# Window attention kernel: first scores in one burst of 32-row matmuls per half image, and a new order of work on all engines

## What is computed

```python
win = x.reshape(B, C, nH, w, nW, w).transpose(0, 2, 4, 3, 5, 1).reshape(B * nH * nW, S, C)
q, k, v = jnp.split(_layernorm(win, ln1_g, ln1_b) @ in_w.T + in_b, 3, axis=-1)   # then split into 8 heads
scores = jnp.einsum('bhsd,bhtd->bhst', q, k) / jnp.sqrt(jnp.float32(dh))
attn = jax.nn.softmax(scores, axis=-1)
o = jnp.einsum('bhst,bhtd->bhsd', attn, v)
win = win + o @ out_w.T + out_b                                                  # y1
h = _layernorm(y, ln2_g, ln2_b)
y = y + jax.nn.silu(h @ fc1_w.T + fc1_b) @ fc2_w.T + fc2_b                       # y2
# second layer, per image: (wo (q k / N) v) is folded into one 128x128 matrix M
out = M @ y2 + d
```

## Time and profile before

| | |
|---|---|
| median of 3 runs | 365.84 us (365.79 to 366.97) |
| profiled execution | 366.59 us, of which the span of the trace is 364.8 us |
| TensorE busy, weight loads busy | 348.3 us (95%), 299.3 us (82%) |
| VectorE busy | 285.1 us (78%) |
| ScalarE busy | 245.6 us (67%) |
| GpSimd busy | 166.9 us (46%) |
| mean granted clock of TensorE | 0.988 |

### The profile page before, as it was taken

The page is one execution under the profiler, slowest core; times in us unless marked ns, Lnnn a source line. Parts: engine busy times, 40 slices in busy tenths (PEclk is TensorE's granted clock), DMA queues, the critical chain, the costliest instruction groups (busy, mean ns, idle before and its releaser), DMA issues. The chain is left out here.

```text
span 364.8 us, 9920 instructions
## 1 busy us (share of the span) xinstructions
PE 348.3 (95%) x3424; PEld 299.3 (82%) x3424; DVE 285.1 (78%) x850; ACT 245.6 (67%) x449; POOL 166.9 (46%) x177
## 2 busy tenths in 40 slices
PE   7899899999999999999999999999999999999875
PEld 6788788888888888888888888878888888878563
DVE  5676888888788878798788888888788878867652
ACT  5557776775959477674968658684877659684360
POOL 6513575444455434635445433646444443622430
PEclk9999999999999999999999999999999999999995
DMA  4242130303222131302123031212123031210011
GB/s 133 67 100 63 33 97 4 91 29 82 76 60 72 29 86 58 86 29 72 63 67 86 14 101 58 70 45 58 58 72 101 0 86 58 60 31 2 0 60 58
DMA packets 31859, 21.99 MB, mean 60 GB/s; under 512 B 22432, under 2 KB 23776, under 8 KB 31840
## 3 DMA queue, kind: packets, MB, share of 16 engines
q1 hardware_dynamic: 31744, 21.62, 21.7%
q10 hardware_dynamic: 96, 0.13, 0.1%
HBM read 4.95 MB, written 4.19 MB: 25 GB/s over the span
## 5 line engine op out<-in xcount | busy, mean ns | idle before, releaser
L526 POOL TENSOR_TENSOR hid_l<-hid,hid_h 128x512 fp32r<-128x512 f32 x30 | 40.4, 1369 | 37.1 <-ACT hid_h L1136 35.3
L706 PE MATMUL p_score<-kd_h,qd_h 128*128 128x128 f32 (+1 forms) x512 | 55.8, 252 | 1.6 <-DMA qd_h<-q_h 1.5
L706 PEld LDWEIGHTS p_score<-kd_h,qd_h 128*128 128x128 f32 (+1 forms) x512 | 49.9, 163 | 6.9 <-DVE row_max L1344 1.7
L1102 ACT ACTIVATE probs<-p_scoreT 128x512 f32<-128x512 f32 x64 | 38.6, 603 | 24.5 <-PE p_scoreT L729 24.4
L1344 DVE TENSOR_REDUCE row_max<-p_score 128x8 f32<-128x512 f32 x64 | 44.0, 687 | 14.1 <-PE p_score L706 14.0
L744 PEld LDWEIGHTS p_attn<-vd,probs 128*64 128x64 f32 x1024 | 36.2, 139 | 16.2 <-issue 9.0
L744 PE MATMUL p_attn<-vd,probs 128*64 128x34 f32 x1024 | 45.4, 244 | 1.7 <-ACT probs L1102 1.7
L531 POOL TENSOR_TENSOR y_l<-y,y_h 128x512 fp32r<-128x512 f32 x15 | 19.3, 1285 | 60.2 <-ACT y_h L1116 60.2
L518 POOL TENSOR_SCALAR kd_l<-k_l,head_a 128x512 fp32r<-128x512 f32 x15 | 23.6, 1572 | 35.7 <-DVE k_l L1326 21.3
L725 PE MATMUL p_scoreT<-qd_h,kd_h 128*128 128x256 f32 x128 | 39.5, 309 | 0.0
L510 POOL TENSOR_TENSOR rstd<-rstd,minus_half 128x4 f32<-128x4 f32 (+1 forms) x33 | 35.5, 1075 | 2.7
(11 more groups left out here) (262 smaller groups left out, 915.5 us busy)
## 6 DMA issues: line engine op xcount, KB each, us to landing
qd_l<-q_l SPq DMA_DIRECT2D x64, 64.0 KB, 2.0
vd<-v_tok SPq DMA_DIRECT2D x64, 64.0 KB, 2.2
qd_h<-q_h SPq DMA_DIRECT2D x62, 64.0 KB, 2.0
out<-out_sb SPq DMA_DIRECT2D x15, 256.0 KB, 2.0
x_in<-in_x SPq DMA_DIRECT2D x14, 256.0 KB, 2.7
x_first<-in_x SPq DMA_DIRECT2D x2, 256.0 KB, 2.8
fc_rows<-in_L_conv_fc_w SPq DMA_DIRECT2D x2, 128.0 KB, 2.6
out<-out_sb SPq DMA_DIRECT2D x2, 128.0 KB, 2.1
```

The source lines that it names most:

```text
L526: pool.tensor_tensor(hid_l[:, t], hid[:, t], hid_h[:, t].bitcast(F32), ALU.subtract).then_inc(hid_low[t], 1)
L706: last = pe.matmul(p_score[0:rows, 2 * KEYS * j:2 * KEYS * (j + 1)], qd_h[:, h.par, j, 2 * KEYS * p:2 * KEYS * p + rows], kd_h[:, h.par, 2 ...
L1102: act.activation(probs[:, p % 2], p_scoreT[:].rearrange("row (win j q) -> row win j q", win=2, j=QUADS), ACT.Exp, scale=SCORE_SCALE).then_ ...
```

## The change

Stage B's first scores of a half are now made in one piece. `p_a`, `p_d` and a bank for the transposed input (`p_n`) become four neighbouring banks, `p_x`; for the length of the burst all four hold scores, a bank for each head pair. A matmul takes the 32 rows of one head pair straight from `q_h` (not from the spread copy), so four neighbours in the list use four different row groups and four different banks. `scores_read` waits for the four maxima before the banks go back to their other users. The maxima and their widened copies get a slot for each pair. Pairs 0, 1 and 3 are widened on VectorE and pair 2 on ScalarE, as before. All lists are reordered.

```diff
-        row_max = sb("row_max", [128, 2, HEADS])
-        max_wide = sb("max_wide", [128, 2, HEADS, KEYS], BF16)
+        row_max = sb("row_max", [128, PAIRS, HEADS])
+        max_wide = sb("max_wide", [128, PAIRS, HEADS, KEYS], BF16)
...
-        p_score = bank("p_score")
+        p_x = ctx.enter_context(nc.psum_tensor("p_x", [128, QUADS, 512], F32))
+        p_a, p_n, p_d = [p_x[:, 0], p_x[:, 1]], p_x[:, 2], p_x[:, 3]
...
+        def score(p):
+
+            return p_x[:, :, 2 * KEYS * p:2 * KEYS * (p + 1)]
...
-            def b_score(h, p):
+            def b_score(h, with_a):
+
+                pe.wait_ge(q_high, h.n())
+                pe.wait_ge(kd_high[0], h.n())
+                pe.wait_ge(kd_high[1], h.n())
+                pe.wait_ge(v_kept, h.n())
+                pe.wait_ge(k_low, h.n())
+                if not h.follows(1):
+                    pe.wait_ge(bias_kept, 1)
+                elif with_a:
+                    pe.wait_ge(xn_tok_set, h.n(-1))
+                if h.second():
+                    pe.wait_ge(ob_kept, 1)
+                for win, columns in ((1, 2 * KEYS), (0, KEYS)):
+                    for p in range(PAIRS):
+                        for j in range(QUADS):
+                            rows = slice(32 * j, 32 * j + 32)
+                            last = pe.matmul(score(p)[0:columns, j], q_h[rows, 2 * KEYS * p:2 * KEYS * p + columns],
+                                             kd_h[rows, h.par, 2 * p + win], start=True, stop=True)
+                last.then_inc(score_ready, 1)
+
+            def scores_read(h):
+
+                for p in range(PAIRS):
+                    pe.wait_ge(max_ready[p], h.n())
...
             def b_max(h, p):
-                dve.wait_ge(score_ready[p], h.n())
-                if p < 2:
-                    if h.follows(1):
-                        dve.wait_ge(max_wide_ready[p + 2], h.n(1))
-                else:
-                    dve.wait_ge(max_wide_ready[p - 2], h.n())
-                dve.tensor_reduce(row_max[:, p % 2], p_score[:].rearrange("row (h k) -> row h k", h=HEADS), AXIS_X, ALU.max
+                dve.wait_ge(score_ready, h.n())
+                if h.follows(1):
+                    dve.wait_ge(max_wide_ready[p], h.n(1))
+                dve.tensor_reduce(row_max[:, p].rearrange("row (j a) -> row j a", a=2),
+                                  score(p).rearrange("row j (a k) -> row j a k", a=2), AXIS_X, ALU.max
                                   ).then_inc(max_ready[p], 1)
...
             def step(loop, b, with_a, with_next, with_c, with_tail, with_d):
...
-                b_score(b, 0)
+                b_score(b, with_a)
```

More of the change, by code:

```diff
@@ L672, in a_q, with a_k, a_v @@
                 pe.wait_ge(xn_low, h.n())
+                if h.follows(2):
+                    pe.wait_ge(v_kept, h.n(1))
+                three_passes(q_bank(h)[:], [weights(Q_)], [(xn_h[:], xn_l[:])]).then_inc(q_ready, 1)
+            def a_k(h):
+                pe.wait_ge(xn_high, h.n())
+                pe.wait_ge(xn_low, h.n())
+                pe.wait_ge(xn_full, h.n())
+                three_passes(k_bank(h)[:], [weights(K_)], [(xn_h[:], xn_l[:])]).then_inc(k_ready, 1)
+            def a_v(h):
+                pe.wait_ge(xn_full, h.n())
                 if h.second():
                     pe.wait_ge(v_kept, h.n(1))
[L675 to L686, removed]
+                else:
+                    pe.wait_ge(q_high, h.n())
+                    pe.wait_ge(q_low, h.n())
                 for p in range(PAIRS):
@@ L690, in a_v, with b_scoreT @@
                 last.then_inc(v_ready, 1)
-            def b_score(h, p):
+            def b_score(h, with_a):
+                pe.wait_ge(q_high, h.n())
+                pe.wait_ge(kd_high[0], h.n())
[18 more added lines that the diff above has]
+                    pe.wait_ge(max_ready[p], h.n())
+            def b_scoreT(h, p):
                 if p == 0:
                     pe.wait_ge(q_high_dma, h.n(times=16 * QUADS))
-                    pe.wait_ge(kd_high[0], h.n())
-                    pe.wait_ge(kd_high[1], h.n())
-                    if h.follows(1):
-                        pe.wait_ge(max_ready[PAIRS - 1], h.n(1))
-                else:
[L702 to L713, removed]
                     pe.wait_ge(q_low_dma, h.n(times=16 * QUADS))
@@ L728, in b_scoreT @@
                 for j in range(QUADS):
[L729 removed]
+                    last = pe.matmul(dst[:, :, j, :], max_wide[:, p, 2 * j:2 * j + 2, :],
                                      neg_ident[:], start=False, stop=j == QUADS - 1, skip_group_check=True)
@@ L877, in step @@
                 a, next_a, c, tail = loop.half(b.c + 1), loop.half(b.c + 2), loop.half(b.c - 1), loop.half(b.c - 2)
-                b_score(b, 0)
+                b_score(b, with_a)
                 if not with_c:
                     a_q(a)
+                    a_k(a)
+                if with_c:
+                    c_transpose(c)
+                if with_tail:
+                    c_fc2(tail)
+                if with_c:
+                    c_project(c)
+                b_scoreT(b, 0)
+                scores_read(b)
                 if with_a and with_c:
                     a_back(a)
[L883 to L896, removed]
                 if with_c:
@@ L900, in step @@
                     c_kv(tail)
[L901 to L906, removed]
+                if with_next:
+                    a_transpose(next_a)
+                b_scoreT(b, 1)
+                b_attn(b, 0)
                 if with_d:
                     d_kvT(loop, -1)
-                b_attn(b, 1)
+                if with_a and with_c:
+                    a_k(a)
+                    a_q(a)
+                b_scoreT(b, 2)
+                if with_d:
+                    d_bT(loop, -1)
+                b_attn(b, 1)
+                if not with_c:
+                    load_weights()
+                if with_c:
+                    c_back(c)
+                b_scoreT(b, 3)
+                if with_d:
+                    d_mT(loop, -1)
+                b_attn(b, 2)
                 if with_a:
@@ L912, in step @@
                 if with_d:
[L913 to L917, removed]
-                    load_weights()
-                if with_next:
-                    a_transpose(next_a)
-                if with_c:
-                    c_back(c)
-                b_attn(b, 2)
-                if with_d:
                     d_final(loop, -1, 0)
-                b_scoreT(b, 3)
                 if with_c:
                     c_fc1(c, 0)
-                    c_fc1(c, 1)
                 if with_d:
                     d_final(loop, -1, 1)
+                if with_c:
+                    c_fc1(c, 1)
                 b_attn(b, 3)
@@ L934, in step @@
                     load_biases()
+                if with_d:
+                    pe.wait_ge(fin_kept[1], loop.image(-1))
             def step_even(loop, more, c):
@@ L1470, in step @@
                 a, next_a, c, tail = loop.half(b.c + 1), loop.half(b.c + 2), loop.half(b.c - 1), loop.half(b.c - 2)
+                b_max(b, 1)
+                b_max(b, 3)
+                if not with_c:
+                    a_k(a)
+                if with_c:
+                    c_o(c)
                 b_max(b, 0)
```

186 lines of the change are left out of this document (93 added, 93 removed).

## The result

The changed kernel is not faster. Its median is 368.94 us (20 runs, 365.76 to 373.98), that of before in the same comparison 366.19 us (20 runs, 365.34 to 367.61); the ratio is 1.0057, 95% interval 1.0033 to 1.0081, so it is 0.6% longer. Predicted were 357.0 us. The profiled execution took 368.75 us, its span is 367.0 us, 2.2 more than the 364.8 of before, and TensorE's mean granted clock is 0.956, where it was 0.988. The time varies more than before, and with the clock: the fastest of the 20 executions had a mean clock of 0.966, one of 371.18 us had 0.938.

What follows compares the result with a forecast made beforehand. TensorE was taken to bound; a loop through `c_fc2` and `hid_l` makes an image 40.55 us instead of 41.76. 7 x 1.2 = 8.4 off 366.59 gives 358.2, the median 0.75 lower: 357, range 343 to 369.

Steps and rivals of the forecast that it cites:

- The burst: The 32 score matmuls at a half's start, in four row groups, take 1.2 us, between bounds of 1.1 and 3.0.
- The wait at `c_fc2`: TensorE waits there for the second `hid_l`: 1.6 us behind even steps, 0.7 behind odd ones.
- VectorE: Same operations; `y2` ready 6.4 us after the burst's start, `c_kv` needing it at 6.5 and 7.4: fits, just.
- rival 2: VectorE takes over: its 34.61 us and 7.15 us of waits per image stay, nothing gained, 365 to 366; chance 0.15.
- The clock: Rival: TensorE's clock falls in the new waits, once per image for some 4 us, 14 us more, 371; chance 0.08.
- The edges: Outside seven images, at the program's start and last half: net change 0, with 1.5 us either way.

Runs made afterwards that it cites:

- the split's run: Changed kernel with the six pair-0 products of `b_scoreT` issued ahead of `c_fc2`, its subtraction of the maxima left behind the projection: 363.36 us, ratio 0.991.
- the five kernels with something put into the wait: Changed kernel with 26 filler matmuls (362.72 us), first `b_scoreT` products moved ahead (363.36), these plus filler and edge edits (359.8), or without filler, two orders (353.81, 354.87).

## Why the prediction was wrong

- **The burst**: taken at 1.2, right in kind; it is 0.83 to the next start.
- **The wait at `c_fc2`**: predicted at 1.6 and 0.7, it is 1.52 and 0.34, put down to `hid_l`, where they were put, the longer one behind even steps. From `c_fc2` to `c_fc2` an odd step was to take 21.49 and an even one 19.06; it is 141.25 - 120.22 = 21.03 and 160.03 - 141.25 = 18.78 (the next `c_fc2` starts at 160.03), so an image at full clock takes 39.81 instead of 40.55. With the third half that is worth 12.9 us, where 8.4 were predicted.
- **VectorE**: its waits fell from 7.15 to 39.81 - 33.76 = 6.05 us per image, so rival 2 did not come. But the split's run shows that `y2` fits with nothing to spare: 0.7 us of TensorE's work moved out of the way brought 0.1.
- **The clock** is the first step that failed: "The waits here are 0.7 and 1.6 with dense work around, so it is unlikely", with a chance of 0.08. It was read from one wait of 1.52 us that the clock survived. The clock fell in 4 of 6 odd steps, at about 1.6 us each, 6.5 us in the profile; in the five kernels with something put into the wait it fell in none of 30 odd steps. The rival's price, 14 us, was twice too high, as it fell in four images and for some 3 us; but it left out the clock at the two ends (next point).
- **The edges** are the second step that failed: "I take 0, with 1.5 either way". They cost 0.5 + 3.1 + 1.4 at the start, 1.1 back in the third half, and 3.6 at the end. Part of that is the clock again: in the second half it fell behind the wait of 2.50 us (a mean of 0.82 for the half, 1.00 before), and of the epilogue's 3.6 some 1.5 go with the fall behind `c_back`. The queue that makes 2.0 of the 2.50 was named in that very step, the copy of v behind weights and a table load, and not priced. TensorE's timeline of the first step and of `c_back`, where no wait stood before, shows the waits that no row of before could, and ScalarE's the queue:

```profile
24.51 0.40 PE L751 MATMUL p_scoreT<-neg_ident,max_wide 128*128 128x128 bf16 x4 [1.91 <-DVE max_wide L1375]
25.91 0.63 PE L668 MATMUL p_x<-ident,x_in 128*128 128x128 f32 x4 [1.01 <-issue]
...
37.53 1.51 PE L723 MATMUL p_x<-kd_h,q_h 32*128 32x128 f32 x32 [2.50 <-issue]
38.98 1.11 PE L782 MATMUL p_c<-ident,o_tok 128*128 128x128 f32 x4
41.55 0.77 PE L620 MATMUL p_c<-o_h,wh 128*128 128x512 f32 x1 [1.46 <-ACT o_h L1144]
...
334.59 1.11 PE L801 MATMUL p_c<-ident,yn_tok 128*128 128x128 f32 x4 [1.91 <-DVE yn_tok L1315]
```

```profile
34.48 0.74 ACT L1047 ACTIVATE wh<-w_full 128x640 fp32r<-128x640 f32 x1
35.23 1.28 ACT L1026 ACT_TABLE_LOAD   x1
36.53 0.20 ACT L1026 ACTIVATE table_sink<-ident 128x1 f32<-128x1 f32 x1
36.64 0.58 ACT L1114 ACTIVATE v_tok<-p_x 128x512 f32<-128x512 f32 x1
```

The sum by the measured terms: the loop and the third half -12.9 at full clock, the falls in the loop +6.5, the start +5.0, the end +3.6, together the 2.2 us of the span. In the profiled execution the falls in the loop and the edges thus took back all that the loop gave; how much of the start is its waits and how much the clock behind them was not separated. What stays open is why the same wait brings the clock down in one odd step and not in the next, and how much of that is the burst's.

## What to carry to other kernels

When a change makes the bounding engine shorter and leaves it a wait, price the wait twice, for the time in it and for the clock behind it, and put work that is ready into it: here filler as well as real work kept the clock in the loop. Work moved into a wait saves its own length only if the next consumer's data comes earlier too. And a pipeline's first and last steps have lists of their own; each wait that the change adds has to be followed through them as through the loop.

## What the hardware showed that was not expected

- 32 matmuls of 32 rows on one row group, back to back, brought TensorE's clock from 1.00 to 0.50 without any idle time (129.86 to 135.00 above), in 11 of 12 steps of the loop; on four row groups at once, 0.83 us of them with 0.34 idle behind (even steps) did not.
- The order of matmuls within a burst hardly matters: to the next start 0.83 us with the row groups changing from one to the next, 0.92 with four neighbours on the same rows, but 2.89 when all use the same.
- Whether the clock falls behind a given wait is not fixed: 16 of 30 with a burst ahead and 1.5 us, 2 of 13 without one and up to 2.0 us. Behind the same wait of 1.91 us at `c_back` it fell in one profile and held in another.
